# A recurrence's divisor: its reciprocal on VectorE, or as a power of minus one on GpSimd, with the final product moved behind the next unit's scans

## The chip, the cores and the metric

The kernel runs on one core of one Trainium2 chip. Its engines are named as the profile names them: PE (TensorE), DVE (VectorE), ACT (ScalarE), POOL (GpSimd) and SP (SyncE, which here only issues transfers). The metric is the time of one execution on the device in microseconds, lower is better.

## What is computed

Two layers over 2048 tokens of 512 channels. Each layer first runs a recurrence over time in both directions ("cond"), then a mixture of experts ("ffn"), and adds the result to x. The reference of the recurrence, cut:

```python
decay = exp(-exp(w))[None, :] * (0.5 + 0.5 * tf)
ek = exp(minimum(k, 30.0)); ekv = ek * v              # k and v are the same array here
# forward scan nf, df and backward scan nb, db of a = a * decay + ekv, b = b * decay + ek
euk = exp(minimum(u + k, 30.0))
num = nf + nb - ekv + euk * v
den = df + db - ek + euk
base = sigmoid(r) * (num / maximum(den, 1e-08))
out = base * (0.8 + 0.2 * tf)
```

Layer 0's ffn has RMS norm, a router to 2 of 8 experts and one shared expert; layer 1's has a softmax gate to 6 of 32 experts and a shared one. num / den does not depend on r, so the kernel makes it for both layers from the same input k, ahead of where it is used.

## The kernel before

The quotient num / den is made in 32 units, each 128 channels by 512 time steps: units 0 to 15 are those of layer 0, units 16 to 31 those of layer 1. All engines run one list of steps, `stages()` (from line 119), and each takes the steps that it has a part in, in the order of the list; semaphores order the engines against each other. Nothing is moved by a scheduler.

One unit n goes like this. SP loads wkK (the input k). ACT makes wkEK = exp(k) and wkEU = exp(u + k) (`k_exp`). DVE clamps wkEK (`k_min`, L1333), POOL makes the product wkEKV (`k_mul`, L1006). DVE scans forward over wkEK into wkFD and over wkEKV into wkFN (`k_fwd`, L1342 and L1346); ACT multiplies both by a gain (L1124, L1126); DVE scans backward (`k_bwd`, L1353, L1356). DVE adds clamped wkEU to wkFD, the divisor (`k_den`, L1363), and makes the numerator's last part (L1366); POOL adds it to wkFN (`k_num`, L1014). DVE takes the reciprocal of wkFD (`k_rec`, L1371) and multiplies (`k_out`, L1378). PE transposes the result through PSUM and ACT stores it in RT (`k_turn`, L1697 and L1143). wkFD and wkFN have two buffers each, wkEK and wkEKV one.

In the first stage (s from 0 to 14, lines 205 to 270, and unit 15 behind it) each step s takes unit s, one token tile of layer 0 and, from s = 7 on, one block of the shared expert. A tile gets `gate` (DVE L1389, reads RT), its sum of squares (`f_sq`, ACT), mean (`f_var` on DVE L1407) and the power of minus a half (`f_var` on POOL, L1020). In the next step `f_hi` (ACT L1182) scales the tile by that power, and stands on ACT ahead of `k_fwd`'s gains; `f_lo` (DVE L1415) makes the float16 remainder. POOL also makes the low halves of some weight pieces (`w_lo`, L1026), and issues adding transfers of finished blocks (L1064).

In the second stage (lines 387 to 434) units 16 to 31 come as halves, `next_half()`: the first half is the scans, the second the rest. The halves stand between the blocks of the shared and the routed experts of layer 0: 27 halves over 39 routed blocks. POOL issues a gather of token rows for each routed block (`gather`, L1054), three blocks ahead. `turn_made()` puts the transposes of a finished unit ahead of the next half. The token rows of layer 1 need all of units 16 to 31.

## Time and profile before

| what | value |
|---|---|
| time, median of 2 runs | 1564.04 us (1561.73 to 1566.35) |
| span of the profiled execution | 1559.5 us |
| PE busy | 1332.1 us (85%) |
| DVE busy | 997.9 us (64%) |
| ACT busy | 738.5 us (47%) |
| POOL busy | 595.8 us (38%) |
| chain that ended last | PE 67%, DVE 21%, issue 5%, ACT 3%, DMA 2% |

A busy share is an average over stages that differ. In the page's 40 slices DVE shows 8 and 9 tenths in the first seven and PE 0 to 7; from the ninth slice on PE shows 9 nearly throughout. The chain's largest DVE line is the reciprocal, L1371, with 5% of the span. The granted TensorE clock lies between 0.6 and 0.9 in slices 3 to 8, and at 0.9 or more from the ninth on but for one slice.

### The profile page before, as it was taken

The page shows a single profiled execution, that of the slowest core. Times are in us where ns is not written, and L with a number is a line of the kernel's source. Part 1 is how long each engine was busy: PE and PEld are TensorE (multiplying, and loading weights), DVE is VectorE, ACT ScalarE, POOL GpSimd, SP SyncE. Part 2 cuts the span into 40 slices and gives each one's busy share as a digit, 9 for nine tenths or more (in the row PEclk, how much of TensorE's full clock was granted, in tenths as well). Part 3 has the DMA queues.
Part 4 walks back from the last instruction along what each step waited for, and adds up shares of the span by engine and source line. Part 5 has one row for each costly group of instructions (what it writes and reads, how often), then busy time and mean ns, then how long its engine had stood idle before and what let it go on. Part 6 is the DMA issues. An engine that isn't in the chain of part 4 may idle for free.

```text
span 1559.5 us, 23674 instructions
## 1 busy us (share of the span) xinstructions
PE 1332.1 (85%) x8228; PEld 808.5 (52%) x8228; DVE 997.9 (64%) x1752; ACT 738.5 (47%) x1259; POOL 595.8 (38%) x462
## 2 busy tenths in 40 slices
PE   0047565599999599899899999999999999999997
PEld 0023252244444365566565666666666666666664
DVE  8999988979897658888545444444444444444222
ACT  4466654645554453441255454444544444454332
POOL 2343443444342343320143444344444444444343
PEclk9987866799999799999999999999999999999999
DMA  3557545678996775541278898988989998898665
GB/s 104 170 163 199 148 115 136 130 195 178 230 239 161 192 224 168 169 132 40 95 188 209 199 210 200 206 201 201 208 192 219 194 205 207 202 208 170 116 105 75
DMA packets 224178, 269.12 MB, mean 173 GB/s; under 512 B 148608, under 2 KB 148736, under 8 KB 223936
## 3 DMA queue, kind: packets, MB, share of 16 engines
q1 hardware_dynamic: 187408, 175.58, 42.5%
q0 software_dynamic: 36656, 92.03, 29.6%
q8 instruction: 70, 1.15, 0.3%
q14 instruction: 44, 0.36, 0.1%
HBM read 167.87 MB, written 70.32 MB: 153 GB/s over the span
## 4 chain that ended last, share of the span: by engine, by line
PE 67%; DVE 21%; issue 5%; ACT 3%; DMA 2%; POOL 0%; SPq 0%; POOLq 0%; DVEq 0%; ACTq 0%
PE psG L1832 38%; PE psO L1881 20%; DVE wkFD L1371 5%; PE psH L1849 3%; DVE wkFD L1353 2%; DMA ST<-W 2%; PE psX L1793 2%; DVE wkFN L1346 2%; DVE wkFD L1342 2%; DVE Wlo L1632 2%; DVE wkFN L1378 1%; DVE wkFN L1356 1%; DVE wkFD L1363 1%; PE psX L1731 1%; DVE H L1651 1%
## 5 line engine op out<-in xcount | busy, mean ns | idle before, releaser
L1832 PE MATMUL psG<-Whi,XSp 128*128 128x352 f16 (+2 forms) x3000 | 671.4, 329 | 11.4 <-issue 9.8
L1832 PEld LDWEIGHTS psG<-Whi,XSp 128*128 128x128 f16 x3000 | 295.3, 100 | 211.7 <-issue 37.5
L1881 PE MATMUL psO<-Whi,HS 128*128 128x512 f16 (+1 forms) x1180 | 390.5, 383 | 0.5 <-DVE OB L1671 0.5
L1832 PE MATMUL psG<-Wlo,XSp 128*128 128x352 f16 (+2 forms) x1500 | 389.0, 329 | 0.0
L1072 POOL DMA_INDIRECT out<-OB,posb x128 | 202.7, 1584 | 416.4 <-ACT OB L1279 412.7
L1632 DVE SCALAR_TENSOR_TENSOR Wlo<-ST,Whi 128x1088 f16<-128x1088 f32 (+1 forms) x116 | 149.6, 1291 | 212.0 <-ACT Whi L1225 204.1
L1651 DVE SCALAR_TENSOR_TENSOR H<-H,psG 128x352 f32<-128x352 f32 (+1 forms) x215 | 105.3, 490 | 242.5 <-ACT H L1244 226.8
L1881 PE MATMUL psO<-Wlo,HS 128*128 128x512 f16 (+1 forms) x590 | 226.3, 384 | 0.0
L1244 ACT ACTIVATE H<-psG 128x352 f32<-128x352 f32 (+1 forms) x215 | 95.3, 443 | 235.0 <-PE psG L1832 226.9
L1832 PEld LDWEIGHTS psG<-Wlo,XSp 128*128 128x128 f16 x1500 | 149.2, 99 | 93.4 <-issue 7.8
L1881 PEld LDWEIGHTS psO<-Whi,HS 128*128 128x128 f16 x1180 | 117.2, 99 | 118.2 <-issue 5.4
L1279 ACT ACTIVATE OB<-psO,WSL 128x512 f32<-128x512 f32 x128 | 88.1, 688 | 173.8 <-PE psO L1881 173.7
L1054 POOL DMA_INDIRECT XG<-xrows,posb x128 | 129.1, 1009 | 103.6 <-DVE posb L1563 55.3
L1225 ACT ACTIVATE Whi<-ST 128x1088 f16<-128x1088 f32 (+1 forms) x116 | 127.4, 1100 | 18.9 <-DMA ST<-W 18.8
L1653 DVE SCALAR_TENSOR_TENSOR H<-H,psG 128x352 f32<-128x352 f32 (+1 forms) x215 | 106.4, 495 | 7.4
L1014 POOL TENSOR_TENSOR wkFN<-wkFN,wkEU 128x512 f32<-128x512 f32 x32 | 40.5, 1266 | 182.2 <-DVE wkEK L1333 171.1
L1661 DVE TENSOR_TENSOR HS<-psH,HS 128x384 f16<-128x384 f32 x160 | 88.1, 550 | 30.2 <-ACT HS L1257 29.9
L1371 DVE RECIPROCAL wkFD<-wkFD 128x512 f32<-128x512 f32 x32 | 107.0, 3344 | 0.0
L1257 ACT CAST HS<-psH 128x384 f16<-128x384 f32 x160 | 75.7, 473 | 59.6 <-PE psH L1849 58.8
L1697 PE MATMUL psX<-C,wkFN 128*128 128x128 f32 x64 | 16.4, 405 | 102.2 <-DVE wkFN L1378 102.2
L1026 POOL TENSOR_TENSOR Wlo<-ST,Whi 128x1024 f16<-128x1024 f32 (+1 forms) x33 | 72.1, 2187 | 67.9 <-ACT Whi L1229 67.9
L1881 PEld LDWEIGHTS psO<-Wlo,HS 128*128 128x128 f16 x590 | 58.2, 99 | 47.7 <-issue 1.7
(219 smaller groups left out, 1550.3 us busy)
## 6 DMA issues: line engine op xcount, KB each, us to landing
ST<-W SPq DMA_DIRECT2D x130, 544.0 KB
ST<-W SPq DMA_DIRECT2D x23, 512.0 KB
slots<-OB SPq DMA_DIRECT2D x39, 256.0 KB
wkK<-fT SPq DMA_DIRECT2D x32, 256.0 KB
xrows<-XG SPq DMA_DIRECT2D x20, 256.0 KB, 3.4
y0rows<-x SPq DMA_DIRECT2D x8, 512.0 KB, 5.3
y0rows<-OB POOLq DMA_DIRECT2D x16, 256.0 KB, 4.7
out<-OB SPq DMA_DIRECT2D x16, 256.0 KB
```

Of the source, the lines that this page charges most:

```text
L1054: G.indirect_dma_start(out=XG[g % 3][:, 0:w], out_offset=None, in_=X[l][:, :], in_offset=bass.IndirectOffsetOnAxis(ap=idx[l][:, j:j + 1], ...
L1072: G.indirect_dma_start(out=Y1[:, :], out_offset=bass.IndirectOffsetOnAxis(ap=idx[1][:, j:j + 1], axis=0), in_=OB[o % 4][:, :], in_offset=N ...
L1225: op = A.activation(st if who == "pool" else hi, st, ACT.Copy, scale=WS)
L1244: A.activation(H32[a][:, 0:F], psG[a][0][:, 0:F], ACT.Tanh, scale=0.5 * UN).then_inc(b_tanh, 1)
L1279: A.activation(OB[o % 4][:, :], psO[bank(o)][:, :], ACT.Copy, scale=scale).then_inc(b_outa, 1)
L1371: V.reciprocal(FD[n % 2][:, :], FD[n % 2][:, :]).then_inc(k_rec, 1)
L1632: op = V.scalar_tensor_tensor(out=Wlo[:, at:at + cw], in0=st, scalar=WS, in1=Whi[:, at:at + cw], op0=ALU.mult, op1=ALU.subtract)
L1651: V.scalar_tensor_tensor(out=H, in0=H, scalar=1.0, in1=g, op0=ALU.add, op1=ALU.mult).then_inc(b_sil, 1)
L1653: V.scalar_tensor_tensor(out=H, in0=H, scalar=(-0.5, 0.5)[l] * XS * UN * UN, in1=u, op0=ALU.mult, op1=ALU.mult).then_inc(b_h, 1)
L1661: V.tensor_tensor(hs(n)[:, 1, 0:w], psH[:, 0:w], hs(n)[:, 0, 0:w], ALU.subtract).then_inc(b_hslo, 1)
L1832: op = M.matmul(o, hx[:, x, q * P:q * P + P], w(half_, off + c, nn), start=first, stop=last)
L1881: op = M.matmul(psO[bank(o)][:, :], hs(n)[:, x, q * P:q * P + P], columns[n](half_, off0 + q * 512, 512), start=(q == 0 and x == 0 and hal ...
```

## The change

The divisor's reciprocal, which DVE made with its own instruction, is made on POOL as a `tensor_tensor` with the power operation and a broadcast column of minus one. That column and the existing one of minus a half become the two columns of one tile, `halves`. On POOL a unit's product for the next unit now stands ahead of its sum, and the power follows the sum. The final product `k_out` of unit n stands behind the scans of unit n + 1, on DVE and in the list, and the transposes follow it; the last unit of each stage keeps its place. The steps of the second stage are arranged the same way.

```diff
--- before.py
+++ after.py
@@ -161,20 +161,19 @@
         yield "k_den", u
         if u + 1 < 32:
             yield "k_min", u + 1
+            yield "k_mul", u + 1
         yield "k_num", u
-        if u + 1 < 32:
-            yield "k_mul", u + 1
+        yield "k_rec", u
         yield from piece
         if u + 2 < 32:
             yield "k_load", u + 2
-        yield "k_rec", u
 
 
     half, made, raised = [32], [], [16]
 
     def turn_made():
         while made:
-            u = made.pop()
+            u = made.pop(0)
             yield "k_turn", u
             if u in (19, 23):
                 yield "k_store", u // 4
@@ -186,11 +185,13 @@
         half[0] += 1
         if second:
             yield from second_half(u)
-            yield "k_out", u
-            made.append(u)
         else:
             yield "k_fwd", u
             yield "k_bwd", u
+        v = u if second else u - 1
+        if v == 31 or not second and v >= 16:
+            yield "k_out", v
+            made.append(v)
 
     def after_half():
 
@@ -221,6 +222,8 @@
         for i in now:
             yield "f_sq", i
         yield "k_bwd", s
+        if s >= 1:
+            yield "k_out", s - 1
         if s >= 1:
             yield "k_turn", s - 1
         for i in turned:
@@ -245,7 +248,6 @@
             yield "h_turn", b - 1
         for i in now:
             yield "f_var", i
-        yield "k_out", s
         for g in range(2):
             if s == 4 * g + 10:
                 yield "r_pos", g
@@ -290,6 +292,7 @@
     yield "f_sq", 10
     yield "f_sq", 11
     yield "k_bwd", 15
+    yield "k_out", 14
     yield "k_turn", 14
     yield "f_turn", 9
     yield "f_lo", 9
@@ -623,7 +626,8 @@
         ones16 = sb("ones16", [P, 128], F16)
         ident16 = sb("ident16", [P, 128], F16)
         ones = sb("ones", [P, 8])
-        half = sb("half", [P, 1])
+        halves = sb("halves", [P, 2])
+        half, minus = halves[:, 0:1], halves[:, 1:2]
         sv = sb("sv", [P, 20])
         rmsw = sb("rmsw", [P, 4])
         rw = [sb("rw0", [P, 4, 8]), sb("rw1", [P, 4, 32])]
@@ -1013,11 +1017,18 @@
                     eng.wait_ge(k_min, n + 2)
                 G.tensor_tensor(FN[n % 2][:, :], FN[n % 2][:, :], EU[n % 2][:, :], ALU.add).then_inc(k_num, 1)
 
+            def k_rec_(n):
+                eng.wait_ge(k_den, n + 1)
+                if n == 0:
+                    eng.wait_ge(s_half, 1)
+                G.tensor_tensor(FD[n % 2][:, :], FD[n % 2][:, :], minus.to_broadcast([P, 512]),
+                                ALU.pow).then_inc(k_rec, 1)
+
             def f_var_(f):
                 eng.wait_ge(f_var, f + 1)
                 if f == 0:
                     eng.wait_ge(s_half, 1)
-                G.tensor_tensor(sm[:, f, 2:3], sm[:, f, 1:2], half[:, :], ALU.pow).then_inc(f_pow, 1)
+                G.tensor_tensor(sm[:, f, 2:3], sm[:, f, 1:2], half, ALU.pow).then_inc(f_pow, 1)
 
             def w_lo(k):
                 l, e, c0, cw, at, who = PIECES[k]
@@ -1088,7 +1099,7 @@
                         in_offset=bass.IndirectOffsetOnAxis(ap=sl0[:, 2 * i + k:2 * i + k + 1], axis=0)
                     ).then_inc(d_pick[i % 2], 16)
 
-            mine = dict(k_mul=k_mul, k_num=k_num_, f_var=f_var_, w_lo=w_lo, gather=gather, pick=pick, down=down)
+            mine = dict(k_mul=k_mul, k_num=k_num_, k_rec=k_rec_, f_var=f_var_, w_lo=w_lo, gather=gather, pick=pick, down=down)
             for what, n in stages():
                 if what in mine:
                     mine[what](n)
@@ -1299,7 +1310,8 @@
                 V.memset(zero[:, :], 0.0).then_inc(s_zero, 1)
                 V.memset(ones16[:, :], 1.0)
                 V.memset(ones[:, :], 1.0)
-                V.memset(half[:, :], -0.5).then_inc(s_half, 1)
+                V.memset(minus, -1.0)
+                V.memset(half, -0.5).then_inc(s_half, 1)
                 for h in H32:
                     V.memset(h[:, :], 0.0)
                 eng.wait_ge(d_const, 5 * 16)
@@ -1366,10 +1378,6 @@
                 V.scalar_tensor_tensor(out=u[:, :], in0=u[:, :], scalar=E30, in1=K[n % 2][:, :], op0=ALU.min,
                                        op1=ALU.mult).then_inc(k_euv, 1)
 
-            def k_rec_(n):
-                eng.wait_ge(k_den, n + 1)
-                V.reciprocal(FD[n % 2][:, :], FD[n % 2][:, :]).then_inc(k_rec, 1)
-
             def k_out_(n):
                 f = FN[n % 2]
                 eng.wait_ge(k_num, n + 1)
@@ -1671,7 +1679,7 @@
                 V.scalar_tensor_tensor(out=OB[o % 4][:, :], in0=psO[bank(o)][:, :], scalar=UN, in1=before[:, :],
                                        op0=ALU.mult, op1=ALU.add).then_inc(b_outv, 1)
 
-            mine = dict(setup=setup, k_min=k_min_, k_fwd=k_fwd, k_bwd=k_bwd, k_den=k_den_, k_rec=k_rec_,
+            mine = dict(setup=setup, k_min=k_min_, k_fwd=k_fwd, k_bwd=k_bwd, k_den=k_den_,
                         k_out=k_out_, x_sum=x_sum, gate=gate, f_var=f_var_, f_lo=f_lo_, logit=logit, r_top=r_top, r_red=r_red_, r_mask=r_mask_,
                         r_wts=r_wts, r_copy=r_copy, r_slot=r_slot, r_place=r_place, hot=hot, places0=places0, table0=table0, table1=table1, w_lo=w_lo, weight=weight, gu=gu,
                         h_turn=h_turn, down=down)
```

DVE, in the first stage, from unit 7's reciprocal to unit 8's backward scans, before (lg, H and sm belong to a tile's logits, a shared block's gated product and a norm's mean; XR is a token tile):

```order
L1371 RECIPROCAL wkFD<-wkFD 128x512
L1425 TENSOR_SCALAR lg<-psG,sm 128x8
L1651 SCALAR_TENSOR_TENSOR H<-H,psG 128x256
L1653 SCALAR_TENSOR_TENSOR H<-H,psG 128x256
L1407 TENSOR_SCALAR sm<-sm 128x1
L1378 SCALAR_TENSOR_TENSOR wkFN<-wkFD,wkFN 128x512
L1342 SCALAR_TENSOR_TENSOR wkFD<-dec,wkEK 128x512
L1346 SCALAR_TENSOR_TENSOR wkFN<-dec,wkEKV 128x512
L1389 SCALAR_TENSOR_TENSOR XR<-XR,RT 128x512
L1353 SCALAR_TENSOR_TENSOR wkFD<-dec,wkFD 128x511
L1356 SCALAR_TENSOR_TENSOR wkFN<-dec,wkFN 128x511
```

And in the changed kernel, whose lines are numbered some 10 higher, from the clamp for unit 8 (L1345) to the tile's remainder behind unit 8's scans (L1423); scans are written as SCALAR_TENSOR_TENSOR in such rows:

```order
L1345 TENSOR_SCALAR wkEK<-wkEK 128x512
L1433 TENSOR_SCALAR lg<-psG,sm 128x8
L1659 SCALAR_TENSOR_TENSOR H<-H,psG 128x256
L1661 SCALAR_TENSOR_TENSOR H<-H,psG 128x256
L1415 TENSOR_SCALAR sm<-sm 128x1
L1354 SCALAR_TENSOR_TENSOR wkFD<-dec,wkEK 128x512
L1358 SCALAR_TENSOR_TENSOR wkFN<-dec,wkEKV 128x512
L1397 SCALAR_TENSOR_TENSOR XR<-XR,RT 128x512
L1365 SCALAR_TENSOR_TENSOR wkFD<-dec,wkFD 128x511
L1368 SCALAR_TENSOR_TENSOR wkFN<-dec,wkFN 128x511
L1386 SCALAR_TENSOR_TENSOR wkFN<-wkFD,wkFN 128x512
L1423 SCALAR_TENSOR_TENSOR XSp<-XR,sm,XSp 128x512
```

The reciprocal is gone, and the final product (L1378 before, L1386 now) stands behind the backward scans instead of ahead of the forward ones.

POOL, the same step, before: sum of unit 7, product for unit 8, a weight piece's low half, the norm's power, and the next unit's sum.

```order
L1014 TENSOR_TENSOR wkFN<-wkFN,wkEU 128x512
L1006 TENSOR_TENSOR wkEKV<-wkEK,wkK 128x512
L1026 TENSOR_TENSOR Wlo<-ST,Whi 128x1024
L1020 TENSOR_TENSOR sm<-sm,half 128x1
L1014 TENSOR_TENSOR wkFN<-wkFN,wkEU 128x512
```

In the changed kernel: product, sum, the new power (L1024), low half, the norm's power, and the next product.

```order
L1010 TENSOR_TENSOR wkEKV<-wkEK,wkK 128x512
L1018 TENSOR_TENSOR wkFN<-wkFN,wkEU 128x512
L1024 TENSOR_TENSOR wkFD<-wkFD,halves 128x512
L1037 TENSOR_TENSOR Wlo<-ST,Whi 128x1024
L1031 TENSOR_TENSOR sm<-sm,halves 128x1
L1010 TENSOR_TENSOR wkEKV<-wkEK,wkK 128x512
```

The new instruction stands ahead of the low half and of the norm's power. ACT's and SP's instructions and their order are unchanged.

## Rows read from the trace of the kernel before

**Rows 1.** Busy time in four stretches: PE, PEld, DVE, ACT, POOL; PEclk, DMA share, GB/s

```profile
73.00:211.00 138.00, 76.63 (x339) 44.69 (x340) 135.64 (x202) 87.75 (x162) 61.42 (x47) 0.80 0.62 165
280.00:320.00 40.00, 29.47 (x121) 13.61 (x120) 35.35 (x37) 19.14 (x37) 17.06 (x14) 0.81 0.66 138
320.00:480.00 160.00, 150.31 (x746) 74.03 (x745) 141.56 (x169) 85.10 (x193) 66.58 (x58) 1.00 0.92 215
480.00:520.00 40.00, 23.15 (x116) 11.22 (x113) 31.40 (x34) 21.80 (x39) 9.67 (x8) 0.88 0.49 152
```

**Rows 2.** Groups by line: shapes and count | busy us, mean ns | idle before

```profile
L1371 DVE RECIPROCAL wkFD<-wkFD 128x512 f32<-128x512 f32 x32 | 107.0, 3344 | 0.0
...
L1006 POOL TENSOR_TENSOR wkEKV<-wkEK,wkK 128x512 f32<-128x512 f32 x32 | 41.5, 1296 | 9.0 <-DVE wkEK L1333 9.0
```

**Rows 3.** One line's instructions: count, shortest/median/longest in ns, first and last start

```profile
L1378 DVE SCALAR_TENSOR_TENSOR wkFN<-wkFD,wkFN x32: 691/693/1936, 20.3 to 500.4; 128x512 f32<-128x512 f32 x32
...
L1020 POOL TENSOR_TENSOR sm<-sm,half x16: 538/996/1021, 77.4 to 226.2; 128x1 f32<-128x1 f32 x16
...
L1014 POOL TENSOR_TENSOR wkFN<-wkFN,wkEU x32: 1252/1264/1332, 17.1 to 497.2; 128x512 f32<-128x512 f32 x32
```

**Rows 4.** Timeline between units 7 and 8: start us, duration us, engine, line

```profile
98.48 1.26 POOL L1014 TENSOR_TENSOR wkFN<-wkFN,wkEU 128x512 f32<-128x512 f32 x1 [7.26 <-DVE wkEK L1333]
...
99.71 1.26 POOL L1006 TENSOR_TENSOR wkEKV<-wkEK,wkK 128x512 f32<-128x512 f32 x1
100.93 2.12 POOL L1026 TENSOR_TENSOR Wlo<-ST,Whi 128x1024 f16<-128x1024 f32 x1
...
103.01 1.00 POOL L1020 TENSOR_TENSOR sm<-sm,half 128x1 f32<-128x1 f32 x1
...
104.04 0.72 ACT L1182 ACTIVATE XSp<-XR,sm 128x512 f16<-128x512 f32 x1 [4.34 <-POOL sm L1020]
...
104.77 0.72 ACT L1124 ACTIVATE wkFD<-wkFD,dcg 128x511 f32<-128x511 f32 x1
...
106.35 1.27 DVE L1353 TENSOR_TENSOR_SCAN wkFD<-dec,wkFD 128x511 f32<-128x511 f32 x1
...
108.72 0.72 DVE L1415 SCALAR_TENSOR_TENSOR XSp<-XR,sm,XSp 128x512 f16<-128x512 f32 x1
...
109.36 0.68 DVE L1363 SCALAR_TENSOR_TENSOR wkFD<-wkEU,wkFD 128x512 f32<-128x512 f32 x1
...
110.08 0.69 DVE L1366 SCALAR_TENSOR_TENSOR wkEU<-wkEU,wkK 128x512 f32<-128x512 f32 x1
110.69 0.42 DVE L1333 TENSOR_SCALAR wkEK<-wkEK 128x512 f32<-128x512 f32 x1
...
111.28 1.27 POOL L1014 TENSOR_TENSOR wkFN<-wkFN,wkEU 128x512 f32<-128x512 f32 x1 [7.27 <-DVE wkEK L1333]
```

**Rows 5.** Timeline: POOL's sums of units 0, 5, 15, and what follows

```profile
17.13 1.26 POOL L1014 TENSOR_TENSOR wkFN<-wkFN,wkEU 128x512 f32<-128x512 f32 x1 [5.43 <-DVE wkEK L1333]
...
72.91 1.26 POOL L1014 TENSOR_TENSOR wkFN<-wkFN,wkEU 128x512 f32<-128x512 f32 x1 [8.42 <-DVE wkEK L1333]
...
210.21 1.25 POOL L1014 TENSOR_TENSOR wkFN<-wkFN,wkEU 128x512 f32<-128x512 f32 x1 [6.32 <-DVE wkEK L1333]
...
214.21 1.11 DVE L1378 SCALAR_TENSOR_TENSOR wkFN<-wkFD,wkFN 128x512 f32<-128x512 f32 x1
...
222.41 1.06 POOL L1020 TENSOR_TENSOR sm<-sm,half 128x1 f32<-128x1 f32 x2 [6.14 <-DVE sm L1407]
```

**Rows 6.** Timeline of POOL in the second stage: two sums and two gathers

```profile
372.12 1.27 POOL L1014 TENSOR_TENSOR wkFN<-wkFN,wkEU 128x512 f32<-128x512 f32 x1 [6.98 <-DVE wkEK L1333]
...
380.99 1.15 POOL L1054 DMA_INDIRECT XG<-xrows,idx  x1 [4.00 <-DMA XSp<-XG]
386.09 1.26 POOL L1014 TENSOR_TENSOR wkFN<-wkFN,wkEU 128x512 f32<-128x512 f32 x1 [3.94 <-DVE wkEK L1333]
...
388.72 0.97 POOL L1054 DMA_INDIRECT XG<-xrows,idx  x1
```

## The prediction

> **What bounds the kernel now.** I read first the busy table by stretch [rows 1], then the costliest groups of the recurrence [rows 2], then what one power and one product cost at their extremes [rows 3], then one step of the first stage in order of time [rows 4], and last where the units lie in time [rows 5, 6].
>
> [rows 1]: from 73 to 211 us, where units 5 to 14 run beside the layer-0 shared blocks, DVE is busy 135.6 of 138 us and PE only 76.6. From 320 to 480 us, where most of units 16 to 31 run beside the routed blocks, PE has 150.3 of 160 and DVE 141.6. So DVE sets the pace of the first stage, and PE, with DVE close behind, of the second. From 520 us on nothing is touched. [rows 2]: the reciprocal on DVE takes 3.344 us, 32 times, 107.0 us in all; a product on POOL takes 1.30 us, and a sum of the same shape 1.26 [rows 3]. [rows 5]: unit 0's sum starts on POOL at 17.13, unit 5's at 72.91 and unit 15's at 210.21, so a unit takes 11.16 us in the first five and 13.73 us on average in the next ten (137.3 over 10).
>
> **The loop that hardly has slack.** [rows 4] is the step between units 7 and 8. DVE ends the clamp; POOL does sum (98.48), product (99.71), the weight piece's low half (100.93), and then the tiny power for a tile's norm (103.01, over at 104.01). ACT waited 4.34 us for that power; then come the tile's scaling (104.04) and behind it, in ACT's order, the gain on the forward scan (104.77, over at 105.49). DVE's backward scan needs that gain; it starts at 106.35. Then backward scans, f_lo, denominator, numerator part, clamp, and POOL's next sum at 111.28. The circle takes 12.80 us and only 0.86 us of it (105.49 to 106.35) is slack. So POOL, though less than half busy, lies on a circle that is almost as long as DVE's own work. Anything that is put on POOL ahead of the norm's power lengthens it.
>
> **The change, part by part.** Let X be what one 128x512 power takes on POOL.
>
> 1. DVE loses the reciprocal: 3.28 us a unit by pitch. Where DVE alone sets the pace that is the gain: units 0 to 4, where no norm's power and no f_hi stand in the circle. DVE would need 7.9 us there (11.16 - 3.28).
>
> 2. POOL gets product, sum, power (in this order), and then the low half and the norm's power. Swapping product and sum costs nothing: both were in the circle. The power of X stands ahead of low half and norm's power, thus fully in the circle of [rows 4].
>
> 3. The final product k_out stands on DVE between the backward scans and f_lo. It was outside the circle (DVE did it while POOL worked); now it is inside, 0.69 us when it runs undisturbed [rows 3]. The circle in units 5 to 14 becomes 12.80 - 0.86 + 0.69 + X = 12.63 + X. Against the 137.3 us that these ten steps take now, the change is 126.3 + 10X - 137.3 = 10X - 11.0 us. It gives nothing even if X is as short as an addition. The two longer steps (tables of the router on DVE) are inside the 137.3; the 3 us that they have more lie beside POOL's part, 6.9 us + X.
>
> 4. There is a second circle: power, k_out (0.69), denominator (0.72), numerator part (0.61), clamp to POOL's start (0.59), product and sum (1.23 each), power: 5.07 + X by the pitches of [rows 4]. In units 0 to 4 the period is the larger of that and 7.9. The five steps change by 5 times (that - 11.16): -16.3 us for X up to 2.8, 5X - 30.5 above.
>
> 5. Unit 15 is waited for: its transposed rows feed the last four tiles. Now k_out starts 4.00 us after POOL's sum does (210.21 to 214.21, [rows 5]); then 2.46 + X after the clamp: X - 1.5 us.
>
> 6. Second stage, 16 units, 13.97 us between two sums of [rows 6] (372.12 and 386.09). DVE gets 3.3 us lighter where PE was the bound: of 240 us between 280 and 520, PE was idle 10.5 + 9.7 + 16.9 = 37.1 us [rows 1], and not all of that was for DVE. For a short X I take 10 us gained. But POOL's queue also holds the gathers of the coming blocks: one stands right behind product and sum (388.72, [rows 6]), and another row shows such a gather waiting 4.00 us for its buffer, so they are issued as soon as they can be. The power comes ahead of them. A gather late by X of 10 us, for a block that PE starts some 14 us later, of which fetch and transpose take most, stalls PE by perhaps half of it. I take 5 us a unit at X = 10, 75 us in 15 units, nothing at X = 4.5. Also k_out and the gated products queued behind it on DVE wait for the same power; this lies beside the gather's wait, and I don't count it twice.
>
> The extra constant (a second column in one tile, a memset on DVE at the start) is one instruction of about 0.1 us under the constants' load: nothing.
>
> **The price of X**, on which all hangs, is not in the trace of before. Bounds: not below the 1.26 us of an addition of the same shape [rows 3]; not above 512 times the one-column power where two follow each other, 1.06 / 2 = 0.53 us [rows 5], or 271 us. (Alone, behind other work, it takes 1.0 us at its median [rows 3].) A column's power costs 0.53 us where a column of addition costs 1.26/512 = 0.0025. That small form must hold a fixed part and a long chain of dependent steps, which a loop over 512 columns can overlap; but if it is made of a logarithm, a product and an exponential, each with several steps, it should still be worth several additions. I take 10 us, eight additions, an estimate that lies nearer (in ratio) to the addition than to the 271; 4.5 to 30 seems as likely around it.
>
> The sum at X = 10, against the profiled execution: units 0 to 4 +19.5; units 5 to 14 +89; unit 15 +8.5; second stage +75: 192 us. The profiled span is 1559.5 and the runs' median 1564.0, 4.5 us more for what lies around it; 1564 + 192 = 1756. At X = 1.26: -16.3 + 1.6 - 0.3 - 10 = -25, or 1539. At X = 4.5: -8 + 34 + 3 + 0 = +29, or 1593. At X = 30: +120 + 289 + 28.5, and POOL itself sets the second stage: it is busy 66.6 of 160 us, 5.8 in 13.97, so a unit takes about 36 us, +22 times 15 = 330, and some 30 of stalls: 2360.
>
> On contention the trace has a row: k_out takes 0.69 us at its median and up to 1.94 beside POOL's work [rows 3]. That supports the Trainium skill (GPSIMD Engine Reference, section 8): the engine shares its SBUF interfaces with VectorE, and a VectorE instruction with two SBUF inputs contends with it. By that rule the gate product of units 5 to 14, which now would lie beside the power, costs some 0.5 us more each, 5 us in all; but it waits there anyway for ACT's gain, so I leave it out of the sum.
>
> **Rivals.**
> A. Power of 4.5 to 30 us: slower, 1593 to 2360, likeliest 1756. For it: 0.53 us for one column. Against: nothing shows the loop. Chance 0.50.
> B. Power nearly as cheap as an addition, 1.3 to 4.5 us. Then the early units gain and the circle of [rows 4] eats it: 1539 to 1593, within 2%. For it: both products of POOL are limited by what they stream, and a power may hide under that. Chance 0.24. The Trainium skill (GPSIMD Engine Reference, section 3.1) gives about 2.6 cycles per element for a two-input elementwise instruction there; the sums of 1.26 us agree, and read as a rule for every such operation it would give the 1539.
> C. Faster by over 2%: X under 1.9 us and the second stage really bound by DVE, so that half to all of PE's 37.1 us of idle time goes: -15 - 18.5 = 1530 down to -15 - 37 = 1512. It decides at X = 1.9 and 16 us gained in the second stage. Against: nothing in these rows says that PE's idle time is DVE's doing, and the price is at its lowest end. Chance 0.11.
> D. The power's loop overlaps little, X above 30: POOL sets everything. At 271 us, 32 x 271 = 8.7 ms, about 10,000 us. Chance 0.15.
>
> **How the numbers follow.** Measurement of this kernel can tell about 2% (31 us) from no change. A and D are slower, 0.65; B is within, 0.24; C faster, 0.11. The time is A's, 1756. The range reaches from the middle of C to just above X = 30: 1525 to 2400; outside are most of D and half of C, 0.2.
>
> **What would show it.** The power's row gives X at once. Right: in units 5 to 14 the sums on POOL start 12.6 + X apart, ACT's tile scaling waits for POOL more than 4.34 us, DVE falls well under 135 of 138 us; in the early units the pitch is 7.9 or 5.1 + X. In the second stage PE waits behind gathers. Wrong: a power outside 4.5 to 30 us; or the pitch of units 5 to 14 well below 12.6 + X, which would mean that the circle through the norm's power is not closed.

## The result, and the profile after

| what | before | after |
|---|---|---|
| time, median of 2 runs each (lowest to highest) | 1564.04 us (1561.73 to 1566.35) | 4046.97 us (4046.06 to 4047.87) |
| ratio to before, with its 95% interval | | 2.5874 (2.5787 to 2.5961) |
| span of the profiled execution | 1559.5 us | 4044.1 us |

The change makes the kernel 2.59 times as slow. The prediction had the direction, but its time (1756 us) and its range (up to 2400 us) were far too low. It comes down to one instruction. These are lines of the profile page of the changed kernel: the engines' busy time, the chain that ended last, and the group of the power (L1024).

```profile
PE 1378.1 (34%) x8228; PEld 825.8 (20%) x8228; DVE 912.7 (23%) x1721; ACT 740.3 (18%) x1259; POOL 3228.9 (80%) x494
...
POOL 46%; PE 25%; issue 22%; DVE 4%; DMA 1%; ACT 1%; POOLq 0%; SPq 0%; ACTq 0%; DVEq 0%
...
L1024 POOL TENSOR_TENSOR wkFD<-wkFD,halves 128x512 f32<-128x512 f32 x32 | 2628.7, 82147 | 0.0
```

A power of 128x512 takes 82.1 us at its mean, where the reciprocal on DVE took 3.34 [rows 2] and a sum of the same shape on POOL takes 1.26 [rows 3]. The 32 of them are 2629 us, more than the 2485 us that the span grew by.

The waits of the whole span (who waited, for whom: us in total, times, longest) show the circle of the prediction closed. DVE's final product waits for the power. ACT's tile scaling (L1193) waits for the tiny power of the norm (L1031), which stands behind the large one on POOL, and DVE's backward scan (L1365) waits for ACT's gain behind it. PE waits for the final product.

```profile
DVE wkFN L1386 <- POOL wkFD L1024: 1642.7, 22, 83.4
...
PE psX L1705 <- DVE wkFN L1386: 1394.6, 16, 104.1
...
ACT XSp L1193 <- POOL sm L1031: 795.1, 10, 85.9
DVE wkFD L1365 <- ACT wkFD L1135: 790.6, 11, 84.3
```

The timeline of one step of the first stage (start, duration, engine, line), the one that answers to [rows 4]:

```profile
558.55 1.27 POOL L1010 TENSOR_TENSOR wkEKV<-wkEK,wkK 128x512 f32<-128x512 f32 x1 [6.84 <-DVE wkEK L1345]
...
561.01 81.95 POOL L1024 TENSOR_TENSOR wkFD<-wkFD,halves 128x512 f32<-128x512 f32 x1
...
642.92 2.13 POOL L1037 TENSOR_TENSOR Wlo<-ST,Whi 128x1024 f16<-128x1024 f32 x1
644.99 0.56 POOL L1031 TENSOR_TENSOR sm<-sm,halves 128x1 f32<-128x1 f32 x1
645.59 0.72 ACT L1193 ACTIVATE XSp<-XR,sm 128x512 f16<-128x512 f32 x1 [84.52 <-POOL sm L1031]
646.21 0.70 ACT L1135 ACTIVATE wkFD<-wkFD,dcg 128x511 f32<-128x511 f32 x1
...
646.95 1.28 DVE L1365 TENSOR_TENSOR_SCAN wkFD<-dec,wkFD 128x511 f32<-128x511 f32 x1 [82.13 <-ACT wkFD L1135]
...
652.40 1.27 POOL L1010 TENSOR_TENSOR wkEKV<-wkEK,wkK 128x512 f32<-128x512 f32 x1 [6.85 <-DVE wkEK L1345]
```

It is the old circle with 82 us put in: 93.85 us from product to product. Where [rows 1] had DVE busy 135.6 of 138 us, these rows of the changed kernel give, for most of units 5 to 15 and for units 16 to 31, PE, PEld, DVE, ACT and POOL busy, then the granted PE clock (full speed is 1), the DMA share and GB/s. POOL is busy 93 and 98% of the time; no other engine is busy for more than 18%.

```profile
465.00:1404.00 939.00, 75.73 (x332) 42.38 (x332) 99.79 (x186) 86.63 (x161) 875.62 (x57) 0.63 0.09 24
1559.00:2900.00 1341.00, 232.96 (x936) 109.23 (x935) 148.82 (x205) 111.49 (x246) 1317.69 (x89) 0.58 0.13 31
```

**Where the 2485 us lie.** POOL's sums mark the units. Those of units 0, 5, 15, 16 and 31 in the changed kernel, by its timeline (units 0, 5 and 15 of before are [rows 5]):

```profile
18.70 1.70 POOL L1018 TENSOR_TENSOR wkFN<-wkFN,wkEU 128x512 f32<-128x512 f32 x1
...
465.05 1.26 POOL L1018 TENSOR_TENSOR wkFN<-wkFN,wkEU 128x512 f32<-128x512 f32 x1
...
1404.46 1.26 POOL L1018 TENSOR_TENSOR wkFN<-wkFN,wkEU 128x512 f32<-128x512 f32 x1
...
1558.80 1.26 POOL L1018 TENSOR_TENSOR wkFN<-wkFN,wkEU 128x512 f32<-128x512 f32 x1
...
2899.58 1.26 POOL L1018 TENSOR_TENSOR wkFN<-wkFN,wkEU 128x512 f32<-128x512 f32 x1 [3.05 <-DVE wkEU L1378]
```

and those of units 16 and 31 before:

```profile
282.30 1.25 POOL L1014 TENSOR_TENSOR wkFN<-wkFN,wkEU 128x512 f32<-128x512 f32 x1 [2.57 <-DVE wkEK L1333]
...
497.16 1.27 POOL L1014 TENSOR_TENSOR wkFN<-wkFN,wkEU 128x512 f32<-128x512 f32 x1 [11.12 <-DVE wkEU L1366]
```

| stretch | before | after | more | the prediction's formula at X = 81.95 |
|---|---|---|---|---|
| start to unit 0 | 17.1 | 18.7 | 1.6 | 0 |
| units 0 to 5 | 55.8 | 446.4 | 390.6 | 5X - 30.5 = 379 |
| units 5 to 15 | 137.3 | 939.4 | 802.1 | 10X - 11.0 = 808 |
| unit 15 to 16 | 72.1 | 154.3 | 82.2 | X - 1.5 = 80 |
| units 16 to 31 | 214.9 | 1340.8 | 1125.9 | 15 (5.8 + X - 13.97) + 30 = 1137 |
| unit 31 to the end | 1062.3 | 1144.5 | 82.2 | 0 |

So with the right price the prediction's own formulas give 1564 + 2405 = 3969 us, 2% below what was measured. Its last line is missing in them: the power of the last unit is waited for with nothing beside it. In the timeline of the changed kernel the last final product waits 83.39 us for it, and PE behind it 81.89 us for the product:

```profile
2982.83 0.69 DVE L1386 SCALAR_TENSOR_TENSOR wkFN<-wkFD,wkFN 128x512 f32<-128x512 f32 x1 [83.39 <-POOL wkFD L1024]
```

That leaves three questions for experiments. Does the price go with the columns, or is there a large fixed part? Do the formulas also hold for a small X, where the prediction placed its rivals? And what does the other half of the change, the moved final product, do by itself?

### The profile page after: what moved, and what is told of

Same layout as the page of the kernel before. It is cut to its first block, busy times and chain, and to the rows that moved or that the text cites. A ratio compares the mean times of both kernels' runs of the same rounds, so it can differ in the third digit from the quotient of the medians.

```text
span 4044.1 us, 23676 instructions
## 1 busy us (share of the span) xinstructions
PE 1378.1 (34%) x8228; PEld 825.8 (20%) x8228; DVE 912.7 (23%) x1721; ACT 740.3 (18%) x1259; POOL 3228.9 (80%) x494
## 4 chain that ended last, share of the span: by engine, by line
POOL 46%; PE 25%; issue 22%; DVE 4%; DMA 1%; ACT 1%; POOLq 0%; SPq 0%; ACTq 0%; DVEq 0%
POOL wkFD L1024 44%; PE psG L1840 14%; PE psO L1889 7%; PE psH L1857 1%; POOL wkEKV L1010 1%; POOL wkFN L1018 1%; DMA ST<-W 1%; PE psX L1801 1%; DVE wkFN L1386 1%; DVE Wlo L1640 1%; POOL Wlo L1037 1%; DVE wkFD L1375 0%; DVE wkEU L1378 0%; PE psG L1739 0%; PE psX L1739 0%
## 5 line engine op out<-in xcount | busy, mean ns | idle before, releaser
L1024 POOL TENSOR_TENSOR wkFD<-wkFD,halves 128x512 f32<-128x512 f32 x32 | 2628.7, 82147 | 0.0
L1840 PE MATMUL psG<-Whi,XSp 128*128 128x352 f16 (+2 forms) x3000 | 685.2, 334 | 118.5 <-issue 98.1
L1889 PE MATMUL psO<-Whi,HS 128*128 128x512 f16 (+1 forms) x1180 | 402.0, 394 | 0.5 <-issue 0.5
L1386 DVE SCALAR_TENSOR_TENSOR wkFN<-wkFD,wkFN 128x512 f32<-128x512 f32 x32 | 29.3, 915 | 1642.7 <-POOL wkFD L1024 1642.7
L1705 PE MATMUL psG<-C,wkFN 128*128 128x128 f32 x64 | 17.3, 424 | 1067.8 <-DVE wkFN L1386 1067.8
L1705 PEld LDWEIGHTS psX<-C,wkFN 128*128 128x128 f32 x64 | 11.4, 216 | 1400.1 <-DVE wkFN L1386 1400.1
L1705 PEld LDWEIGHTS psG<-C,wkFN 128*128 128x128 f32 x64 | 11.2, 212 | 1075.9 <-DVE wkFN L1386 1075.6
L1365 DVE TENSOR_TENSOR_SCAN wkFD<-dec,wkFD 128x511 f32<-128x511 f32 x32 | 42.0, 1313 | 790.6 <-ACT wkFD L1135 790.6
L1659 DVE SCALAR_TENSOR_TENSOR H<-H,psG 128x352 f32<-128x352 f32 (+1 forms) x215 | 105.8, 492 | 326.7 <-ACT H L1255 312.4
L1010 POOL TENSOR_TENSOR wkEKV<-wkEK,wkK 128x512 f32<-128x512 f32 x32 | 45.8, 1432 | 103.3 <-DVE wkEK L1345 103.2
```

Source lines behind the costliest of these rows:

```text
L1010: G.tensor_tensor(EKV[:, :], EK[:, :], K[n % 2][:, :], ALU.mult).then_inc(k_ekv, 1)
L1024: G.tensor_tensor(FD[n % 2][:, :], FD[n % 2][:, :], minus.to_broadcast([P, 512]), ALU.pow).then_inc(k_rec, 1)
L1386: V.scalar_tensor_tensor(out=f[:, :], in0=FD[n % 2][:, :], scalar=1e8, in1=f[:, :], op0=ALU.min, op1=ALU.mult).then_inc(k_out, 1)
L1659: V.scalar_tensor_tensor(out=H, in0=H, scalar=1.0, in1=g, op0=ALU.add, op1=ALU.mult).then_inc(b_sil, 1)
L1705: op = M.transpose(bank_[:, q * P:q * P + P], FN[n % 2][:, q * P:q * P + P], ident)
L1840: op = M.matmul(o, hx[:, x, q * P:q * P + P], w(half_, off + c, nn), start=first, stop=last)
```

## The experiments

Diffs are against the changed kernel unless another is named. A pitch is the distance of two units' sums on POOL; the first number is the mean in units 0 to 5, the second in units 5 to 15, the third in units 16 to 31. Before they are 11.16, 13.73 and 14.32 us, after 89.3, 93.9 and 89.4. A time is the median of a kernel's runs, its ratio is to the kernel before, measured beside it, with the 95% interval. Pitches, waits and timelines are from one profiled execution. The kernels are called e1 to e11 in the text. Those with 64 and 8 columns, e4 and e8, ran once each.

### The price of the power: 64 and 8 columns

```diff
-                G.tensor_tensor(FD[n % 2][:, :], FD[n % 2][:, :], minus.to_broadcast([P, 512]),
+                G.tensor_tensor(FD[n % 2][:, 0:64], FD[n % 2][:, 0:64], minus.to_broadcast([P, 64]),
                                 ALU.pow).then_inc(k_rec, 1)
```

> The changed kernel with the power over 64 of the 512 columns (the others stay un-inverted and the final product takes min(divisor, 1e-8), so the quotient is left out). If the price grows in proportion to columns from 0.55 us at 1 to 81.95 at 512 (0.159 us a column), the instruction takes 10.6 us; that is the price that was forecast. By the prediction's own sum with X = 10.6: +22 in units 0 to 4, +95 in units 5 to 14, +9 for unit 15, +79 in the second stage, about 1770 us. If the price has a large fixed part or works in blocks, the instruction is far from 10.6 us.

The other run has 8 columns in the same place.

> As e4_power64 with the power over 8 columns (quotient left out). Proportional in columns with the fixed part of 0.39 us: 0.39 + 8 x 0.159 = 1.7 us. If the loop works in blocks of many columns, 8 columns cost about as much as 1 (0.55 us) or as 64 (about 10.6 us).

The power's instructions (count: shortest/median/longest in ns, first and last start) with 64 columns and with 8 (the 81.95 us of all 512 stand in the step shown above):

```profile
L1024 POOL TENSOR_TENSOR wkFD<-wkFD,halves x32: 10536/10552/11484, 22.1 to 701.6; 128x64 f32<-128x64 f32 x32
```

```profile
L1024 POOL TENSOR_TENSOR wkFD<-wkFD,halves x32: 1639/1666/2604, 20.7 to 515.1; 128x8 f32<-128x8 f32 x32
```

From 8 to 64 columns it is (10.55 - 1.67) / 56 = 0.159 us a column, from 64 to 512 it is (81.95 - 10.55) / 448 = 0.159: straight, with some 0.4 us fixed. The norm's one-column power fits (0.4 + 0.16 against 0.55 us in the changed kernel). A column's power costs as much as 65 columns of sum (0.159 against 1.26 / 512 = 0.0025). No part of it becomes cheaper with length.

With 64 columns the kernel (e4) takes 1777.69 us, within half a per cent of the expected time, with pitches of 17.88, 22.53 and 18.92. X is 10.55 us there, close to the 10 us that the prediction took. Two of its terms come out well (units 5 to 15: +88.0 against 10X - 11.0 = 94.5; unit 15: +9.3 against 9.1). One is too small (units 0 to 5: +33.6 against 22.3). Units 16 to 31 gave +69 and the stretch behind them +13, together +82, where 79 were expected for units 16 to 31 alone; the 13 fit the exposed last power, 10.55 us, that the formulas lack. So the sum came out at X = 10 nearly as it did at 82, in part because its misses are of opposite sign. With 8 columns (e8) the time is 1584.31 us and the pitches 10.25, 15.76 and 14.28. The early units gain 0.9 us each, but units 5 to 15 lose 2.0, 20 us in all, where 10X - 11.0 gives 6 at this X: at a small X something else works.

### The small X: a product in the power's place

```diff
-                                ALU.pow).then_inc(k_rec, 1)
+                                ALU.mult).then_inc(k_rec, 1)
```

> The changed kernel with a plain product by a column of one in place of the power (the divisor is left un-inverted and the final product takes min(divisor, 1e-8), so the quotient is left out). POOL's added instruction then costs X = 1.23 us of pitch instead of 82. If the circle through POOL, the norm's power, ACT's gain and DVE's backward scans sets the first stage, units 5 to 15 start 12.63 + 1.23 = 13.9 us apart (13.73 on average before) in spite of DVE being 3.3 us lighter, the first five 7.9 us, and the time is about 1539 us. If DVE alone set the pace, the pitch would fall to about 10 us and the time to about 1510 us.

This kernel, e1, took 1582.76 us, a ratio of 1.0137 (1.0094 to 1.0180), with pitches of 11.01, 15.68 and 13.86. Expected were 1539. DVE lost a 3.34 us instruction per unit, POOL got one of 1.04, and the early units gained 0.15 us each instead of 3.26. The second kernel of this pair, e2, also puts the norm's power ahead of the stand-in and of the low half, which takes both out of the circle of [rows 4]:

```diff
+        for i in norms:
+            yield "f_var", i
         yield "k_rec", u
         yield from piece
```

> As e1_product, with one more edit: the tile's norm (mean on DVE, power of minus a half on POOL) stands right behind the clamp and the sum, ahead of the stand-in and of the weight piece's low half. The circle loses the stand-in (1.23) and the low half (2.07): 13.86 - 3.30 = 10.6 us pitch in units 5 to 15, about 33 us less than e1_product, some 1506 us. If the circle is not what sets e1_product, the two are equal within 5 us.

e2 took 1576.53 us, ratio 1.0084 (1.0060 to 1.0108), pitches 11.01, 15.30 and 14.09, against 1506 expected; it lies 6 us below e1, whose runs spread over 14. Neither the circle through the norm's power nor DVE's own work set the pace here; both expectations fell.

### The move by itself

The reciprocal goes back to DVE, where it stands behind the clamp; all else stays as in the changed kernel.

```diff
+            def k_rec_(n):
+                eng.wait_ge(k_den, n + 1)
+                V.reciprocal(FD[n % 2][:, :], FD[n % 2][:, :]).then_inc(k_rec, 1)
```

> The changed kernel's order, with the reciprocal back on DVE (3.34 us): only the move of the final product behind the next unit's scans and the swap of product and sum are left. The circle becomes 12.80 - 0.86 + 0.69 = 12.6 us and DVE's own work 12.8 - 0.5 (the final product no longer lies beside POOL's low half, 0.69 instead of 1.2 us) = 12.3: within 5 us of 1564 us, a little faster if anything. The rival, that the move costs much of the 2483 us itself, would show here as a time well above 1600 us.

This kernel, e3, took 1579.65 us, ratio 1.0098 (1.0076 to 1.0119), pitches 10.95, 15.43 and 14.59, where a time within 5 us of 1564 was expected. Units 5 to 15 lose nearly as much as in e1 (15.43 and 15.68), with the reciprocal on DVE, which points to the move. The waits from 100 to 228 us of this kernel name the place:

```profile
PE psX L1709 <- DVE wkFN L1390: 55.2, 8, 8.4
...
ACT HT L1200 <- PE psG L1732: 28.1, 9, 4.2
DVE lg L1437 <- PE psG L1743: 16.9, 8, 2.7
```

PE stands at the transposes of the last unit (L1709) until the moved final product is there. Only then come the shared block's products, the tile's transposes (L1732) and its logits (L1743), because in the list `k_turn` stands ahead of `gu_pe` and `f_turn`. DVE then waits for the logits, ahead of the next unit's scans. That is a third circle: final product, PE's queue, ACT's copy HT, logits, DVE. The next kernel, e5, undoes only this, with the turn of unit s - 1 behind the block's products (against e3):

```diff
-        if s >= 1:
-            yield "k_turn", s - 1
 ...
         if b >= 0:
             yield "gu_pe", b
+        if s >= 1:
+            yield "k_turn", s - 1
         for i in turned:
             yield "f_turn", i
```

> e3_moved_only with one more edit: in the first stage the transposes of unit s-1 (PE, and ACT's store) stand behind the shared block's gate and up products instead of ahead of them. In e3_moved_only PE waited 55 us in eight steps at these transposes for the final product that now comes behind the scans, with the block's products queued behind it, and DVE in turn waited 17 us for the logits. If that queue is what the move costs, the pitch of units 5 to 15 falls from 15.4 back to about 13.5 us on average and the time from 1580 to about 1561 us. If the cost is elsewhere (the order on DVE or POOL), it stays at 1580.

e5 took 1560.99 us, ratio 0.9988 (0.9971 to 1.0005), pitches 10.95, 13.63 and 14.03: as expected, the loss is gone. The same waits, in the same stretch:

```profile
PE psX L1709 <- DVE wkFN L1390: 29.5, 8, 8.1
...
ACT HT L1200 <- PE psG L1732: 3.8, 7, 2.0
DVE lg L1437 <- PE psG L1743: 3.2, 2, 2.0
```

The clock does not explain it: the mean granted TensorE clock from 100 to 228 us is 0.74 of full speed before, 0.75 in e3 and 0.69 in e5, so the faster of the two had the lower one.

The same turn, given to e2, is e6:

> e2_product_norm_first (a plain product stands in for the power, so the quotient is left out; the norm stands ahead of it) with the transposes behind the shared block's products, as in e5. Now neither the circle through the norm's power (10.6 us) nor PE's queue should hold DVE, whose own work is 9 to 10 us a step: pitch about 11.5 us on average in units 5 to 15 instead of 15.3, some 38 us less than e2_product_norm_first, about 1539 us. That is what a POOL instruction as cheap as a product could have brought. If PE's queue isn't the cause, it stays at 1576.

e6 took 1565.46 us, ratio 1.0016 (0.9997 to 1.0036), pitches 11.01, 14.04 and 14.22. It is 11 us faster than e2 where 38 were expected, and still no faster than before, with 3.3 us less for DVE in each unit. The third circle is shorter here but not gone. These are DVE's waits for the logits from 74 to 212 us (most of units 5 to 15), in e6 and in the kernel before:

```profile
DVE lg L1433 <- PE psG L1739: 16.7, 9, 2.2
```

```profile
DVE lg L1425 <- PE psG L1731: 0.5, 1, 0.5
```

In e1 the same wait has 39.3 us. From the end of the final product over PE's transposes, ACT's copy and the logits back to DVE one step of e6 takes 4.6 us (109.84 to 114.45). In e5 DVE spends 3.34 us of such a stretch in the reciprocal; without it DVE stands for 2.2 us there.

And e5 with the norm's power early, the reciprocal on DVE, is e7:

> A whole kernel: the reciprocal on DVE, the final product behind the next unit's scans, the norm ahead of POOL's low half, the transposes behind the shared block's products. DVE's own work sets the pace; the final product no longer lies beside POOL's low half (0.7 instead of 1.2 us), so a step takes 12.3 instead of 12.8 us: 5 to 8 us less than the kernel before, about 1557 us. If second-stage costs of the move remain, no gain.

e7 took 1563.61 us, ratio 0.9998 (0.9982 to 1.0015), pitches 10.95, 13.91 and 14.10: the expected 5 to 8 us did not come. With the reciprocal on DVE neither of the two mended orders, e5 and e7, is clear of the time before.

### Why taking 3.3 us from DVE gives nothing

One unit of before and one of e1 in the timeline (DVE and POOL alone), among the early units, where nothing else is in the circle. Before:

```profile
51.45 3.34 DVE L1371 RECIPROCAL wkFD<-wkFD 128x512 f32<-128x512 f32 x1
51.70 1.26 POOL L1014 TENSOR_TENSOR wkFN<-wkFN,wkEU 128x512 f32<-128x512 f32 x1 [8.95 <-DVE wkEK L1333]
52.92 1.26 POOL L1006 TENSOR_TENSOR wkEKV<-wkEK,wkK 128x512 f32<-128x512 f32 x1
...
55.51 1.22 DVE L1342 TENSOR_TENSOR_SCAN wkFD<-dec,wkEK 128x512 f32<-128x512 f32 x1
56.64 1.20 DVE L1346 TENSOR_TENSOR_SCAN wkFN<-dec,wkEKV 128x512 f32<-128x512 f32 x1
```

With the product in place of the power:

```profile
51.06 1.23 DVE L1354 TENSOR_TENSOR_SCAN wkFD<-dec,wkEK 128x512 f32<-128x512 f32 x1
51.11 2.24 POOL L1010 TENSOR_TENSOR wkEKV<-wkEK,wkK 128x512 f32<-128x512 f32 x1 [5.76 <-DVE wkEK L1345]
53.31 1.25 POOL L1018 TENSOR_TENSOR wkFN<-wkFN,wkEU 128x512 f32<-128x512 f32 x1
53.38 2.27 DVE L1358 TENSOR_TENSOR_SCAN wkFN<-dec,wkEKV 128x512 f32<-128x512 f32 x1 [1.09 <-POOL wkEKV L1010]
54.53 1.95 POOL L1024 TENSOR_TENSOR wkFD<-wkFD,halves 128x512 f32<-128x512 f32 x1
55.57 1.99 DVE L1365 TENSOR_TENSOR_SCAN wkFD<-dec,wkFD 128x511 f32<-128x511 f32 x1
```

Before, POOL's two instructions lie under the reciprocal, each at its own 1.26 us, and the scans behind it take 1.2. Without the reciprocal they lie beside scans. The product started 0.05 us behind a scan and takes 2.24 us, about the scan's 1.23 and then its own; the next scan takes 2.27 us beside the sum, and so on: one at a time. From 51.06 to 57.56, in 6.5 us, go three scans and three instructions of POOL whose own lengths are 3.7 and 3.6 us: they stand nearly in a row. (The fourth scan, L1368, lies beside nothing here; elsewhere in e1 it takes up to 3.07 us.) The long reciprocal had been the cover under which POOL's work was free.

Summed over DVE's rows of units 0 to 5, before: scans, gate products and final products are 1.5 us longer than by themselves, and DVE never waits. In e1 they are 11.1 us longer and DVE waits 4.5 us, 3.3 of them for POOL's product: together 14.1 us more, of 16.7 that the five reciprocals took.

If that is so, taking POOL's instructions away, or making them small, must give back what the lighter DVE promised. Two kernels do it, e9 against e6 and e10 against e9:

```diff
-                G.tensor_tensor(FD[n % 2][:, :], FD[n % 2][:, :], minus.to_broadcast([P, 512]),
+                G.tensor_tensor(FD[n % 2][:, 0:1], FD[n % 2][:, 0:1], minus,
```

> e6_product_turn_later with the stand-in cut to one column: no engine makes a reciprocal or anything like it (the quotient is left out). DVE's own work in units 0 to 4 is 7.9 us a unit, yet e6's pitch there is 11.0. In e6 POOL's product, sum and stand-in no longer lie beside the one-input reciprocal but beside DVE's scans, and each shows one of the two at 2.2 us instead of 1.2: they exclude each other. If that is the cause, dropping one of three such instructions gives about 1 us: pitch 10.0 in units 0 to 4. If a circle through POOL (5.1 us + 1.2) or DVE alone set the pace, it would be 7.9.

```diff
-                G.tensor_tensor(EKV[:, :], EK[:, :], K[n % 2][:, :], ALU.mult).then_inc(k_ekv, 1)
+                G.tensor_tensor(EKV[:, 0:8], EK[:, 0:8], K[n % 2][:, 0:8], ALU.mult).then_inc(k_ekv, 1)
 ...
-                G.tensor_tensor(FN[n % 2][:, :], FN[n % 2][:, :], EU[n % 2][:, :], ALU.add).then_inc(k_num, 1)
+                G.tensor_tensor(FN[n % 2][:, 0:8], FN[n % 2][:, 0:8], EU[n % 2][:, 0:8], ALU.add).then_inc(k_num, 1)
```

> e9_nothing_instead with POOL's product and sum over 8 columns instead of 512 (the rest of the product tile is zero, the rest of the sum is left out). Nothing of POOL is left to exclude DVE's scans: pitch in units 0 to 4 of 7.9 us, the figure that the prediction took for a reciprocal removed, 2 us less than e9_nothing_instead; the low halves of weight pieces in units 5 to 14 remain. If exclusion is not the cause, e9 and e10 have the same pitch.

e9 took 1546.07 us, ratio 0.9881 (0.9844 to 0.9917), with pitches of 10.27, 13.34 and 13.56. e10 took 1521.19 us, ratio 0.9731 (0.9706 to 0.9756), with 8.83, 11.93 and 13.91. Among the early units each step is in the direction that exclusion gives and of about its size: 0.74 us for the stand-in, where 1 was expected, and 1.4 for product and sum, where 2 were. e10 does not reach the 7.9 us. In its first five units DVE waits 3.8 us for ACT, and one scan lies beside POOL's low half (2.62 us, at 27.38); from unit 0's first scan (17.27) to unit 1's (24.24), without either, it takes 7.0 us. With only one column left in the reciprocal's place (e9) 0.9 of the 3.3 us arrive.

Units 5 to 15 are not explained by POOL alone. In e6, against before, DVE's scans and products there are 10 us longer, and DVE waits 20 us more, 17 of them for the logits; both together eat most of the 33 us that the reciprocals took. In e10 DVE still waits 16 us in that stage, 13 of them for the logits.

In e10, POOL's product of 8 columns takes 0.20 us with no scan beside it (at 33.51) and 1.18 beside one, where it is held up for the length of the scan (timeline of e10, DVE and POOL):

```profile
33.51 0.20 POOL L1010 TENSOR_TENSOR wkEKV<-wkEK,wkK 128x8 f32<-128x8 f32 x1 [4.58 <-DVE wkEK L1346]
...
42.74 1.23 DVE L1355 TENSOR_TENSOR_SCAN wkFD<-dec,wkEK 128x512 f32<-128x512 f32 x1
42.78 1.18 POOL L1010 TENSOR_TENSOR wkEKV<-wkEK,wkK 128x8 f32<-128x8 f32 x1 [8.77 <-DVE wkEK L1346]
```

What sets scan and reciprocal apart could be the number of SBUF inputs or the operation. The traces have instructions of one operation on either side. In e1 the gate product, a SCALAR_TENSOR_TENSOR with two SBUF inputs, takes 0.67 us alone and 1.46 beside POOL. The shared blocks' products are the same operation with one input in SBUF and one in PSUM. In the first 520 us of e1, where some 20 of the 55 at this line lie beside POOL's sums and products, none takes longer (count: shortest/median/longest in ns):

```profile
L1659 DVE SCALAR_TENSOR_TENSOR H<-H,psG x55: 387/420/422, 106.4 to 513.5; 128x256 f32<-128x256 f32 x55
```

By these rows it goes with the second SBUF input; no kernel changed that alone.

The last kernel, e11, turns it round: e5, with the reciprocal on DVE, and a third full-width instruction on POOL under it (the product for the next unit, made once more behind the sum).

```diff
+            def k_rec_(n):
+                if n + 1 < 32:
+                    eng.wait_ge(k_ekw, n + 2)
+                    G.tensor_tensor(EKV[:, :], EK[:, :], K[(n + 1) % 2][:, :], ALU.mult).then_inc(k_ekv, 1)
```

> The kernel of run e5 (reciprocal on VectorE, turns behind the shared block's products; 1561 us, units 10.95 us apart among 0 to 5 and 13.63 among 5 to 15), with one instruction more on GpSimd in each unit: the product for the next unit is made twice, the second time behind the sum, where the changed kernel has its power. Nothing of the result changes. Theory (GpSimd's full-width work is free as long as it lies beside the reciprocal, which reads one SBUF input, and costs its own length beside scans): product, sum and second product take 3.7 us, of which 3.3 lie beside the reciprocal, and at most some 0.4 us a unit come out of the cover. Early pitch 10.95 to 11.4; units 5 to 15 up to 1.2 us longer through the norm's power, 13.6 to 14.9; total 1562 to 1575. Rival (each GpSimd instruction costs VectorE its length wherever it stands, or is paid for by the scans that wait for it): early pitch 12.2, units 5 to 15 at 14.9, units 16 to 31 0.5 to 1.2 longer, total 1580 to 1600.

e11 took 1576.62 us, ratio 1.0116 (1.0075 to 1.0157), pitches 11.56, 14.72 and 14.46. A unit among the first five, DVE and POOL alone:

```profile
54.44 3.35 DVE L1386 RECIPROCAL wkFD<-wkFD 128x512 f32<-128x512 f32 x1
54.60 1.26 POOL L1011 TENSOR_TENSOR wkEKV<-wkEK,wkK 128x512 f32<-128x512 f32 x1 [8.00 <-DVE wkEK L1348]
55.82 1.26 POOL L1023 TENSOR_TENSOR wkFN<-wkFN,wkEU 128x512 f32<-128x512 f32 x1
57.04 1.26 POOL L1028 TENSOR_TENSOR wkEKV<-wkEK,wkK 128x512 f32<-128x512 f32 x1
57.70 1.69 DVE L1357 TENSOR_TENSOR_SCAN wkFD<-dec,wkEK 128x512 f32<-128x512 f32 x1
59.31 1.19 DVE L1361 TENSOR_TENSOR_SCAN wkFN<-dec,wkEKV 128x512 f32<-128x512 f32 x1
```

All three lie beside the reciprocal at their own length and don't lengthen it. The third ends at 58.30, 0.6 us into the scan that starts at 57.70, and that scan takes 1.69 us in place of 1.19. The early pitch grows by 0.61 us to 11.56, above the expected 11.4 and half of the rival's growth of 1.2. Units 5 to 15 lose 1.1 us each, inside the expected range but near the rival's 14.9 too. There the weight piece's low half (L1040) is pushed out from under the reciprocal and lies beside a scan, where both take 3 us:

```profile
95.05 3.04 POOL L1040 TENSOR_TENSOR Wlo<-ST,Whi 128x1024 f16<-128x1024 f32 x1
96.10 3.07 DVE L1361 TENSOR_TENSOR_SCAN wkFN<-dec,wkEKV 128x512 f32<-128x512 f32 x1
```

Units 16 to 31 are 0.4 us apart more than in e5, just under the rival's 0.5. The total lies 1.6 us above the upper end of what was expected and 3 us under the rival's range. By the sizes this run falls between the two; the rows above decide it, since POOL's three instructions and the reciprocal keep their lengths while they lie beside each other, and what sticks out is paid for by the scans.

## Why the prediction was wrong

**The price of X: the step that failed.** The prediction bounded X between 1.26 and 271 us and took 10, "eight additions", since a loop over 512 columns should overlap the long chain behind one column. It took 81.95 us. Of the half microsecond of the one-column power 0.4 are fixed, as supposed, but 0.16 are the column, and every further column costs the same 0.16: no overlap of the columns shows. The true value lay inside the bounds but in rival D, which got 0.15, and the range stopped at X = 30. The choice between the two ends leaned on an idea of how the loop ought to run, for which no row spoke; the trace's only row of this operation said half a microsecond for one column. The direction was right, but with little credit: it was given 0.65, and by the prediction's own sums every price above 4.5 us leads to it. Rival B's page, the Trainium skill (GPSIMD Engine Reference, section 3.1), gives about 2.6 cycles per element for a two-input elementwise instruction. The runs bear it out for sum and product (1.26 us for 512 columns), and not for the power, which takes about 65 times as long.

**Steps 2, 3, 4 and 5, for a large X: right.** The power stands whole in both circles. Units 5 to 15 came out within 1% of 10X - 11.0, units 0 to 5 within 3%, and unit 15's exposure within 2 us, at X = 82; at X = 10.55 the first was 7% too large, unit 15's right within 1 us, and the early units' 5X - 30.5 was 11 us too small.

**Step 6: right in form, one thing forgotten.** POOL sets the second stage once X is large; 1137 us were worked out and 1125.9 measured. The exposed power behind the last unit, 82 us, was left out, although step 5 had the same thing for unit 15. The 5 us a unit at X = 10, put down to late gathers, came out in its size only (4.6 in the kernel with 64 columns); no run parts the gathers from the other waits. The text on the change says that ACT's order stays the same, which is so in the first stage only: in the second, ACT's store of a unit's transposes stood ahead of the next unit's gains (376.75 and 377.96 us, before) and stands behind them in the changed kernel (1846.98 the gain, 1917.51 the store).

**Step 1: wrong at a small X.** "Where DVE alone sets the pace that is the gain: units 0 to 4", 3.28 us a unit. With a cheap instruction on POOL (e1, e6) the early units gained 0.15 us, with one column (e9) 0.9, and with all of POOL's instructions made small (e10) 2.3. In the changed kernel the 82 us hide this.

**The sentence on contention: the wrong verdict.** The prediction named the Trainium skill (GPSIMD Engine Reference, section 8: the engine shares SBUF interfaces with VectorE, and a VectorE instruction with two SBUF inputs contends), priced it at 0.5 us a unit for one gate product, and left it out. The runs bear the page out and give the size: by e1's and e10's timelines sum, product and scan exclude each other for their whole length. It meets all four scans, each of which reads two SBUF inputs, while the reciprocal reads one. The question to ask was what lay beside the instruction that was removed. [rows 3] had the signs: the final product at 0.69 us alone and up to 1.94, the one-column power at 1.00 us where in the changed kernel, beside an idle DVE, it takes 0.55 at its median.

**Step 3's missing part.** The move of the final product was costed at 0.69 us in the circle of [rows 4]. It also holds up PE's queue, where the turn stands ahead of the tile's logits: +17 us in units 5 to 15 of e3, none of it left in e5. Without the reciprocal the same way round makes DVE wait 39 us in e1 and still 17 in e6. In the changed kernel the 82 us hide this.

**The rivals.** B (cheap power, within 2%) and C (faster) both supposed a price like that of e1's stand-in, 1.04 us. That kernel takes 1582.76 us, 1.4% more than before: inside B's 1539 to 1593, but far from the 1539 that B's formula gives at this price. C's second stage, with PE's idle time for DVE, did not appear: units 16 to 31 gain 7 us in e1, 11 in e9 and 6 in e10 over 15 pitches, near the 10 that step 6 took and under C's 16.

## What to carry to other kernels

Before an operation is moved to another engine, its price there has to be known for its shape; where the trace has only a one-column form, a price that grows with every column is the case to plan for, until a run says otherwise. Before a long instruction is taken from VectorE, look at what GpSimd does beside it: here the reciprocal, with one SBUF input, was a cover under which GpSimd's sums and products cost nothing, and beside the scans, with two, they cost their whole length. Look also at what other chains it covers: without it VectorE stood waiting for the logits. And a final step that is moved behind other work also moves what waits for it in a third engine's queue; follow that queue to what stands behind it.

## What was not expected of the hardware

- The power on POOL costs 0.159 us a column on 128 partitions, 81.95 us for 512, with 0.4 us fixed; a product of the same shape with the same broadcast column took 1.04 us.
- POOL's sum and product and a DVE scan, which reads two SBUF inputs, exclude each other nearly whole: 1.26 us became 2.24, a scan's 1.19 became 2.27, and an instruction of 8 columns took 1.18 us instead of 0.20. Beside the reciprocal, and beside a product with one of its two inputs in PSUM, neither changed.
- The slow power does not hold up DVE in the same way: in the changed kernel the scan beside its start takes 1.92 us, and the one behind it, wholly beside the power, its usual 1.19. The power of this step starts at 561.01 and the first scan ends 2.12 us later; in another step the power starts at 1651.88, the scan at 1652.56, and the scan again ends 2.12 us behind the power's start. So the power shuts a scan out for its first 0.9 us and not for the other 81. These are DVE's rows of its timeline:

```profile
561.21 1.92 DVE L1354 TENSOR_TENSOR_SCAN wkFD<-dec,wkEK 128x512 f32<-128x512 f32 x1
563.05 1.19 DVE L1358 TENSOR_TENSOR_SCAN wkFN<-dec,wkEKV 128x512 f32<-128x512 f32 x1
```

Why the exclusion holds for the whole of a sum and not for most of a power, and whether it goes by the reads or the writes, was not tried.
